# First stage of a cross-attention and expert kernel put in another order: key weights, row statistics, second normalised pair and the values of three batches

## What is computed

```python
def layer(x, ctx):
    q = layernorm(x) @ w_q.T + b_q             # 16 heads of 16 features
    k, v = split(ctx @ w_kv.T + b_kv)          # per batch: 77 keys, 77 values
    attn = softmax(q k^T / sqrt(16))           # per head, over the 77 keys
    x = x + (attn v) @ w_out.T + b_out
    # then 8 experts of 1024 hidden units, two per row, with a capacity per expert
    h = silu(rows_of_expert @ fc1_w.T + fc1_b)
    y = h @ fc2_w + fc2_b
    return x + layernorm_affine(layernorm(x) + gated sum of y)
```

## Time and profile before

| | |
|---|---|
| time, median of 3 runs | 838.27 us |
| lowest to highest | 837.16 to 839.23 us |
| the profiled execution's own time | 840.41 us |
| its span, first to last instruction | 838.6 us |
| mean granted TensorE clock | 0.905 of full |
| busy: TensorE | 699.2 us (83% of the span) |
| busy: VectorE | 583.7 us (70%) |
| busy: GpSimd | 435.0 us (52%) |
| busy: ScalarE | 395.3 us (47%) |

### The profile page before, as it was taken

One profiled execution on the slowest core, in us unless ns is written; L12 is line 12 of the kernel. 1 busy time (PEld: TensorE's weight loads), 2 busy tenths in 40 slices (PEclk: granted clock), 3 DMA queues, 4 the chain that ended last, 5 costly groups with the idle time before them and its releaser, 6 DMA issues.

```text
span 838.6 us, 16510 instructions
## 1 busy us (share of the span) xinstructions
PE 699.2 (83%) x5636; PEld 662.2 (79%) x5637; DVE 583.7 (70%) x1177; ACT 395.3 (47%) x899; POOL 435.0 (52%) x480
## 2 busy tenths in 40 slices
PE   3599999999999703499999995999969999999600
PEld 2489999899889602499999995999969999999600
DVE  2879888888877599375566666768657566764278
ACT  1255555555555312254455454555535444653264
POOL 3644554554653246625544656557556545542456
PEclk9599999999999855599999996999989999999855
DMA  9301101101101150214424545345443443332375
GB/s 291 126 14 39 36 29 39 38 28 38 39 29 36 52 156 0 60 32 101 91 41 101 102 100 107 52 101 106 101 104 52 95 91 52 53 46 26 35 231 175
DMA packets 55334, 63.91 MB, mean 76 GB/s; under 512 B 9296, under 2 KB 50512, under 8 KB 55120
## 3 DMA queue, kind: packets, MB, share of 16 engines
q0 software_dynamic: 15360, 21.31, 15.9%
q1 hardware_dynamic: 34784, 40.96, 14.9%
q10 hardware_dynamic: 5104, 0.44, 0.5%
HBM read 38.96 MB, written 23.72 MB: 75 GB/s over the span
## 4 chain that ended last, share of the span: by engine, by line
PE 79%; DVE 9%; issue 4%; DMA 3%; POOL 2%; ACT 1%; SPq 0%; DVEq 0%; ACTq 0%; POOLq 0%
PE banks L753 17%; PE banks L755 17%; PE banks L754 17%; PE banks L862 9%; PE banks L849 5%; PE banks L837 5%; PE banks L967 2%; PE banks L920 2%; POOL oh_id L531 2%; DMA sum_rows<-y_sb,slot_ids 1%; DVE z L1413 1%; PE banks L875 1%; DMA wv_sb<-in_wvT 1%; PE banks L782 1%; PE banks L910 1%
## 5 line engine op out<-in xcount | busy, mean ns | idle before, releaser
L509 POOL DMA_INDIRECT sum_rows<-y_sb,slot_ids x80 | 128.6, 1607 | 193.0 <-ACT y_sb L702 166.5
L712 ACT ACTIVATE hraw<-banks,b_now 128x256 f32<-128x256 f32 x320 | 132.5, 474 | 101.6 <-PE banks L755 101.5
L753 PE MATMUL banks<-xT_hi,w_hi 128*128 128x256 f32 x560 | 163.9, 293 | 0.2
L755 PE MATMUL banks<-xT_hi,w_lo 128*128 128x256 f32 x560 | 160.7, 287 | 0.0
L754 PE MATMUL banks<-xT_lo,w_hi 128*128 128x256 f32 x560 | 160.6, 287 | 0.0
L753 PE MATMUL banks<-w_hi,h_hi 128*128 128x256 f32 x528 | 148.9, 282 | 2.7 <-issue 2.7
L754 PE MATMUL banks<-w_lo,h_hi 128*128 128x256 f32 x528 | 148.6, 281 | 0.0
L755 PE MATMUL banks<-w_hi,h_lo 128*128 128x256 f32 x528 | 148.5, 281 | 0.0
L1357 DVE CAST h_hi<-hraw 128x512 fp32r<-128x512 f32 x160 | 75.6, 472 | 62.3 <-ACT hraw L712 62.0
L1359 DVE TENSOR_TENSOR h_lo<-hraw,h_hi 128x512 fp32r<-128x512 f32 x160 | 112.0, 700 | 5.5
L753 PEld LDWEIGHTS banks<-xT_hi,w_hi 128*128 128x128 f32 x560 | 108.9, 194 | 7.2 <-issue 7.2
(11 more groups left out here) (194 smaller groups left out, 1465.9 us busy)
## 6 DMA issues: line engine op xcount, KB each, us to landing
w1raw<-in_w1T SPq DMA_DIRECT2D x8, 1024.0 KB, 6.9
w2raw<-in_w SPq DMA_DIRECT2D x8, 1024.0 KB, 6.4
xn_rows<-xn SPq DMA_DIRECT2D x32, 128.0 KB, 1.7
sum_rows<-xn SPq DMA_DIRECT2D x32, 128.0 KB, 1.8
out<-z SPq DMA_DIRECT2D x16, 256.0 KB, 2.2
res<-sum_rows SPq DMA_DIRECT2D x7, 512.0 KB, 7.3
X<-in_x SPq DMA_DIRECT2D x2, 1280.0 KB, 14.2
xg<-xn_rows,slot_ids POOLq DMA_INDIRECT x80, 3.5
```

The costliest lines, as they stand in the source:

```text
L509: g.indirect_dma_start(sum_rows, bass.IndirectOffsetOnAxis(ap=slot_ids[:, st, 1, q:q + 1], axis=0), y_sb[:, u, q, :], None, bounds_check=N ...
L712: a.activation(hraw[:, j // 2, j % 2, :], banks[:, j // 2, (j % 2) * 256:(j % 2 + 1) * 256], ACT.Silu, bias=b1_now[:, (c // SPE) % 2, j:j ...
L753: t_.matmul(o, a_hi, b_hi, start=first, stop=False)
L755: return t_.matmul(o, a_lo, b_hi, start=False, stop=last)
```

## The change

- **Loads.** The key weights count on `load_ctx` instead of sharing a semaphore with the value weights. The order becomes context, keys, x tiles 0 to 3, query weights, value weights, output weights, the rest of x.
- **Keys.** TensorE waits for context and key weights only. Products go to banks PT and PV. ScalarE writes `kT_hi` directly from PSUM with the bias, VectorE makes `kT_lo` from PSUM, bias and `kT_hi` in one instruction; the tile `kT` and its rounding copy are gone.
- **Row statistics.** VectorE starts with the statistics of pair 0, then the low part of the query weights, then the normalisation of pair 0, then the statistics of pair 1; key and value work follows.
- **Second pair.** VectorE's `normalise_first(1)` is gone; GpSimd does it with two `centre` and two `scale` behind `spread_lo(0)`, followed by `bias(0)`, and only then the low keys of batches 1 to 3.
- **Values.** Before the first step only batch 0's values are made, biased and split. The products of batches 1 to 3 stand on TensorE behind the spreading of batch 0, between steps 0 and 1; their bias adds follow on VectorE there, their high and low parts in the hook between steps 1 and 2. The spreading of batch 0 goes round two banks instead of four.
- **ScalarE.** An exponential on a small tile comes early; the high query weights come before the keys; the copy of the key mask comes behind the first transposed pair.

```diff
-        V_BANKS = (PT, PV, TR, PJ)
+        V_BANKS = (PT, PV)
+
+        def v_products(b):
+
+            return banks[0:NK, (TR, PJ)[b // 2], (b % 2) * D:(b % 2 + 1) * D]
...
             sp.dma_start(ctx_sb[:], ctxT.rearrange("(c p) b k -> p c (b k)", p=P)).then_inc(load_ctx, 16)
-            sp.dma_start(wk_sb[:], wkT.rearrange("(c p) o -> p c o", p=P)).then_inc(load_wkv, 16)
+            sp.dma_start(wk_sb[:], wkT.rearrange("(c p) o -> p c o", p=P)).then_inc(load_ctx, 16)
             sp.dma_start(X[:, 0:4, :], x_t[:, 0:4, :]).then_inc(load_x[0], 16)
-            sp.dma_start(wv_sb[:], wvT.rearrange("(c p) o -> p c o", p=P)).then_inc(load_wkv, 16)
             sp.dma_start(wq_sb[:], wqT.rearrange("(c p) o -> p c o", p=P)).then_inc(load_wq, 16)
+            sp.dma_start(wv_sb[:], wvT.rearrange("(c p) o -> p c o", p=P)).then_inc(load_wv, 16)
+            sp.dma_start(wo_sb[:], woT.rearrange("(c p) o -> p c o", p=P)).then_inc(load_wo, 16)
             for n, (a, b) in enumerate(((4, 12), (12, 22), (22, NT))):
                 sp.dma_start(X[:, a:b, :], x_t[:, a:b, :]).then_inc(load_x[n + 1], 16)
-            sp.dma_start(wo_sb[:], woT.rearrange("(c p) o -> p c o", p=P)).then_inc(load_wo, 16)
...
             rstd_first(0)
-            pool.wait_ge(sem("kT_split"), 2 * DC)
+            rstd_first(1)
+            pool.wait_ge(sem("kT_split"), DC)
             spread_lo(0)
-            rstd_first(1)
...
+            pool.wait_ge(sem("xn1T_done"), 1)
+            for w in range(2):
+                centre(xn1[:, w, :], 2 + w, mv1[:, w, 0:1], "xn1_centred")
+            pool.wait_ge(sem("xn1_centred"), 2)
+            for w in range(2):
+                scale(xn1[:, w, :], rstd1[:, w:w + 1], "xn1_made")
+            pool.wait_ge(load_small, 16 * 4)
+            bias(0)
             for b in range(1, NB):
                 spread_lo(b)
...
+            act.wait_ge(sem("half_made"), 1)
+            a.activation(silu_warm[:], minus_half[:, 0:1], ACT.Exp)
+            act.wait_ge(load_wq, 16)
+            a.activation(wq_hi[:], wq_sb[:], ACT.Copy).then_inc(sem("w_hi_ready"), 1)
             act.wait_ge(load_small, 16 * 4)
             for f in range(DC):
                 act.wait_ge(sem("kT_done"), f + 1)
-                a.activation(kT[:, f, :], banks[:, f, 0:NB * NK], ACT.Identity, bias=bk_sb[:, f:f + 1])\
+                a.activation(kT_hi[:, f, :], banks[:, (PT, PV)[f], 0:NB * NK], ACT.Identity, bias=bk_sb[:, f:f + 1])\
                     .then_inc(sem("kT_made"), 1)
...
             first_layernorm(0)
-            act.wait_ge(sem("v_made"), NB)
-            a.activation(v_hi[:], v_sb[:], ACT.Copy).then_inc(sem("v_hi_made"), 1)
+            act.wait_ge(sem("masks_made"), 3)
+            a.activation(key_of_row_r[:], key_of_row[:], ACT.Copy).then_inc(sem("key_rows_made"), 1)
+            act.wait_ge(sem("v_made"), 1)
+            a.activation(v_hi[:, 0, :], v_sb[:, 0, :], ACT.Copy).then_inc(sem("v_hi_made"), 1)
             queries(0)
...
+            def later_values(b):
+                if b == 2:
+                    act.wait_ge(sem("v_made"), NB)
+                    a.activation(v_hi[:, 1:NB, :], v_sb[:, 1:NB, :], ACT.Copy).then_inc(sem("v_hi_made"), 1)
+
+            attention_steps(act, step, later_values)
...
-            pe.wait_ge(load_ctx, 16)
-            pe.wait_ge(load_wkv, 32)
+            pe.wait_ge(load_ctx, 32)
...
-            for b in range(NB):
+
+            def values_product(b):
                 for c in range(DC):
...
-            pe.wait_ge(sem("kT_made"), DC)
             first_layernorm(0)
+            pe.wait_ge(load_wv, 16)
+            values_product(0)
             pe.wait_ge(sem("wq_split"), 1)
             queries(0)
-            pe.wait_ge(sem("v_made"), NB)
...
                         spread(0, j, banks[0:JW, V_BANKS[j % len(V_BANKS)], 0:D])
+                    pe.wait_ge(sem("v_made"), 1)
+                    for n in range(1, NB):
+                        values_product(n)
...
+            def keys_lo(f):
                 dve.wait_ge(sem("kT_made"), f + 1)
-                v.tensor_copy(kT_hi[:, f, :], kT[:, f, :]).then_inc(sem("kT_split"), 1)
+                v.scalar_tensor_tensor(kT_lo[:, f, :], banks[:, (PT, PV)[f], 0:NB * NK], bk_sb[:, f:f + 1],
+                                       kT_hi[:, f, :].bitcast(f32), ALU.add, ALU.subtract)\
+                    .then_inc(sem("kT_split"), 1)
+
+            def values_biased(b):
+                dve.wait_ge(sem("v_done"), 1 if b == 0 else NB)
+                v.tensor_tensor(v_sb[:, b, :], v_products(b), bv_sb[0:NK, :], ALU.add).then_inc(sem("v_made"), 1)
+
+            def values_lo(b, n, made):
+                dve.wait_ge(sem("v_hi_made"), made)
+                v.tensor_tensor(v_lo[:, b:b + n, :], v_sb[:, b:b + n, :], v_hi[:, b:b + n, :].bitcast(f32), ALU.subtract)\
+                    .then_inc(sem("v_lo_made"), 1)
+
             dve.wait_ge(load_x[0], 16)
             row_stats(0)
             dve.wait_ge(sem("st1_made"), 2)
             aggregate(0)
...
             dve.wait_ge(sem("w_hi_ready"), 1)
             split(wq_hi, wq_lo, wq_sb, "wq_split")
+            normalise_first(0)
+            row_stats(1)
+            dve.wait_ge(sem("st1_made"), 4)
+            aggregate(1)
             dve.wait_ge(load_small, 64)
...
+            keys_lo(0)
             first_lo(0)
+            keys_lo(1)
+            values_biased(0)
             dve.wait_ge(sem("masks_made"), 3)
             for f in range(DC):
                 spread_keys(0, f)
...
             queries_lo(0)
-            row_stats(1)
-            dve.wait_ge(sem("st1_made"), 4)
-            aggregate(1)
-            normalise_first(1)
+            values_lo(0, 1, 1)
             dve.wait_ge(load_x[1], 16)
...
                 if u == 0:
+                    if i == 0:
+                        dve.wait_ge(sem("xn1_made"), 4)
                     aggregate(i + 2)
...
                     split(wo_hi, wo_lo, wo_sb, "wo_split")
+                    for n in range(1, NB):
+                        values_biased(n)
+                if b == 2:
+                    values_lo(1, NB - 1, 2)
                     for n in (2, 3):
                         dve.wait_ge(load_x[n], 16)
```

More of the change, by code:

```diff
@@ L414, in _, with bias, centre, scale @@
             rstd_first(0)
-            pool.wait_ge(sem("kT_split"), 2 * DC)
+            rstd_first(1)
+            pool.wait_ge(sem("kT_split"), DC)
             spread_lo(0)
-            rstd_first(1)
+            def bias(j):
+                if within(j, PAIRS):
+                    pool.wait_ge(sem("xn1_made"), 2 * j + 2)
+                    for v in range(2):
+                        xt = X[:, ds(2 * j + v, 1), :].rearrange("p a d -> p (a d)")
+                        g.tensor_tensor(xt, xt, bo_sb[:], ALU.add).then_inc(sem("x_biased"), 1)
+            def centre(out, tile, mean, name):
+                rows = X[:, ds(tile, 1), :].rearrange("p a d -> p (a d)")
+                g.tensor_tensor(out, rows, mean.to_broadcast([P, D]), ALU.subtract).then_inc(sem(name), 1)
+            def scale(out, rstd, name):
+                g.tensor_tensor(out, out, rstd.to_broadcast([P, D]), ALU.mult).then_inc(sem(name), 1)
+            pool.wait_ge(sem("xn1T_done"), 1)
[6 more added lines that the diff above has]
+            bias(0)
             for b in range(1, NB):
@@ L440, in _ @@
                    allow_small_or_imprecise_dtypes=True).then_inc(sem("route_consts"), 1)
[L442 to L458, removed]
             def step(i, u):
@@ L658, in step @@
                                  ACT.Copy).then_inc(sem("logits_made"), 1)
-            attention_steps(act, step)
+            def later_values(b):
[3 more added lines that the diff above has]
+            attention_steps(act, step, later_values)
             router_exp(1, LATE)
@@ L755, in mm3 @@
                 return t_.matmul(o, a_lo, b_hi, start=False, stop=last)
-            pe.wait_ge(load_ctx, 16)
-            pe.wait_ge(load_wkv, 32)
+            pe.wait_ge(load_ctx, 32)
             for f in range(DC):
                 for c in range(DC):
-                    m = t_.matmul(banks[:, f, 0:NB * NK], wk_sb[:, c, f * P:(f + 1) * P], ctx_sb[:, c, :],
+                    m = t_.matmul(banks[:, (PT, PV)[f], 0:NB * NK], wk_sb[:, c, f * P:(f + 1) * P], ctx_sb[:, c, :],
                                   start=(c == 0), stop=(c == DC - 1))
                 m.then_inc(sem("kT_done"), 1)
-            for b in range(NB):
+            def values_product(b):
                 for c in range(DC):
-                    m = t_.matmul(banks[0:NK, 2 + b // 2, (b % 2) * D:(b % 2 + 1) * D],
-                                  ctx_sb[:, c, b * NK:(b + 1) * NK], wv_sb[:, c, :], start=(c == 0), stop=(c == DC - 1))
+                    m = t_.matmul(v_products(b), ctx_sb[:, c, b * NK:(b + 1) * NK], wv_sb[:, c, :],
+                                  start=(c == 0), stop=(c == DC - 1))
                 m.then_inc(sem("v_done"), 1)
```

(18 more changed lines are left out.)

14 lines of the change are left out of this document (3 added, 11 removed).

## The result

| | median, us | lowest to highest | ratio to before, 95% interval |
|---|---|---|---|
| before (4 runs beside it) | 837.71 | 836.49 to 839.23 | |
| after (4 runs) | 830.85 | 830.14 to 831.60 | 0.9919 [0.9902, 0.9935] |

The change makes the kernel 6.9 us faster: 833.0 was forecast, with a range of 829.5 to 837.0. The profiled execution took 830.14 us, its span is 828.4, the mean granted clock 0.916 (before 0.905).

The account below looks back on a forecast made before the run. The front was taken as bound by VectorE and its order, with TensorE at half clock, and attention from about 48 us by TensorE. Terms −4.65 − 2.15 + 1.5 = −5.3 us gave a median of 833.0, range 829.5 to 837.0.

Parts of the forecast that it names:

- Start: First loads and key products: products start at 5.9 instead of 10.1 us, alone off the path; `rstd` there at 10.35.
- Normalising pair 0: VectorE's two `xn`: 0.36 us each without GpSimd beside them, instead of 1.27; done from 11.35 to 12.1.
- `xn` costs 1.27 by itself: Rival on VectorE's normalising: `xn` is no cheaper without GpSimd's `KH_lo` beside it; +1.8 us, 834.8; chance 10%.
- Spreading: Keys spread by VectorE and GpSimd from 15.3 us, taking turns, ending at 19.25; turns cost 0.4 us.
- Queries at half clock: First queries on TensorE, from 15.0 us: taken to last 2.94 us, with `q_hi` done at 18.85.
- Pair 1 on GpSimd: GpSimd normalises pair 1 from 19.25 in four pieces of 0.59 us, ready at 22.0, hidden by 1 us.
- Between the steps: Between steps 0 and 1: rounds over two banks +1.0 us, twelve value products 5.1; tile 1 scores at 34.0, −4.65.
- Step 1 and the clock: Attention step 1: clock full from 33.9 us, saving 2.65; VectorE's biases cost 0.5; together −2.15, step 2 at 41.45.
- Hook behind step 1: Before step 2's `vals`: ScalarE's copy and VectorE's `v_lo` delay them, leaving TensorE standing; +1.5 us, between 0 and 2.5.
- second spell at half clock: Rival: the pause of 1.5 us drops the clock again for 6.85 us, costing 3.4; 836.4; chance 17%.
- stay at 1.2 GHz: Rival for slower, from 34.0 us on: clock stays low; 843.0 us if it rises at 54; chance 6%.
- the default of half clock: Rival at the first key products: started earlier, they run at half clock and end at 13.7; 834.6 us; chance 5%.

Follow-up runs that it names:

- again: The changed kernel profiled and measured once more, unaltered: 830.41 us, 0.9912 of the kernel before.
- the loads alone: Kernel before with only the key weights counted on the context's semaphore, so key products need not wait for the value weights: 834.89 us, 0.9962.
- loads and statistics: Kernel before with key weights counted apart from value weights, and pair 0's row statistics ahead of VectorE's two rounding copies: 832.94 us, 0.9943.
- the value products in front: Changed kernel with the value products of batches 1 to 3 behind the first queries instead of between steps 0 and 1: 830.48 us, 0.9910.
- the padded pair: Kernels before and after, each with nine useless 128-column products at TensorE's very start, shifting the later code: 830.72 and 823.61 us.
- the padded kernel with the same nine: Changed kernel with late value work in idle time, nine useless products in TensorE's early waits, nine more at its start: 821.94 us, 0.9813.

## Why the prediction was right, point by point

| | predicted | after | again |
|---|---|---|---|
| first key product | 5.9 | 5.72 | 5.74 |
| `wq_lo` starts | 10.6 | 10.01 | 10.53 |
| two `xn` | 0.72 | 0.73 | 0.73 |
| scores of tile 0 | 20.25 | 18.37 | 19.30 |
| pair 1 transposed | 23.05 | 20.86 | 22.24 |
| scores of tile 1 | 34.0 | 30.80 | 32.83 |
| step 1 lasts | 7.45 | 7.42 | 7.42 |
| scores of tile 2 | 41.45 | 38.22 | 40.25 |
| step 2, over the 6.38 of before | +1.5 | +1.35 | +1.33 |

**Start: right in its times, incomplete in what it was worth.** In the new order the statistics wait for x alone (8.26), as said. That the shared semaphore had cost the old order 3.2 us, through VectorE's rounding of the keys, was not seen. The first profile was lucky in its query weights: in the ten profiles with the new order of loads, `wq_lo` starts between 10.01 and 11.18, and 10.01 is this one.

**Normalising pair 0: right.** The rival *`xn` costs 1.27 by itself* is refuted twice, by 0.73 for two here and by 0.72 for pair 1 on VectorE, while with the loads alone the same two cost 2.54 beside `KH_lo`, and with loads and statistics one ahead of it cost 0.40 and the next beside it 1.30.

**Spreading: mis-sized.** "GpSimd to 16.5, VectorE 17.25, GpSimd 18.5, VectorE 19.25" assumed turns with GpSimd first. In both profiles VectorE's two `KH_hi` ran through at 1.49 to 1.50, and GpSimd's two took 3.93 and 3.96, 1.46 more than alone, which is just the length of the two `KH_hi` ("alone" is loosely said: the 2.47 of before ran beside `xn`, and it was `xn` that waited). So they do exclude each other, but VectorE's second followed its first without a turn. The bound of step 0 moved from `q_lo` to `KH_lo`.

**Queries at half clock: wrong.** They ran at 1.00 in the profile shown first (13.70 to 15.4, 0.28 each), where 2.94 us at half clock had been taken. The clock was 1.00 up to 19.9. So `q_hi` and `q_lo` came early and `KH_lo` was the last to end. It started at 14.08 (again: 14.98) where 15.3 was forecast, which gives 1.2 (0.3) of the 1.9 us (0.95) by which tile 0 was better than the sum said; the rest is the missing turn and the early `q_lo`.

**Pair 1 on GpSimd: the right time, no worth.** It was ready at 20.6 (22.0 was forecast), ahead of its use, but VectorE would have had the room.

**Between the steps: right.** Twelve products took 4.72 us where 5.1 was forecast, the blocks went in rounds. From pair 1's transposes to the scores of tile 1 passed 9.94 and 10.59 us (predicted 10.95).

**Step 1 and the clock: right in length; the reason went deeper.** The clock was full before the step's scores in both profiles. What the prediction did not see is that the value products bought this: without them step 1 takes 9.1 to 9.9 us. With products without use added in the idle time it took 7.32 us in one profile and 8.79 in the other.

**Hook behind step 1: right.** +1.35 us, TensorE waiting 1.12 for `vals`, and it goes when the copy goes.

**Rivals.** No second spell at half clock followed the pause at 40.5, and the clock did not stay at 1.2 GHz. The first products ran at 1.00, 0.53 us each against 0.49 before, so the default of half clock that the Trainium skill names ("TensorE: Matmul & The Clock Gate", section "What's actually happening") did not meet them. Half clock did come soon behind them in some profiles of this front (0.51 between 12.8 and 16.3 us with the value products in front, scores of tile 0 at 19.78 instead of 18.37), but 1.15 of these 1.4 us stood there already at the first transposes (12.64 against 11.49), behind later query weights.

The forecast's mechanism held; its size was too small in one term. Up to the scores of tile 1 it had −4.65 us, and the profiles have −7.86 and −5.83; step 1 (−2.17 where −2.15 was said) and step 2 were right. The gain was 6.9 instead of 5.3 us.

Between tile 3 and the end the two profiled executions differ by another 1.5 us (10.2 in the span, 8.7 at tile 3); the profiled execution of before, 840.41, also lay 2.7 us above its median. In the padded pair, where the expert stage takes 402.6 us in both, the gain is 6.8 us at tile 3, 6.8 in the span (828.7 to 821.9) and 7.1 in the medians: the change's gain is that of the front. What stays open is why the clock holds in one execution of a front and not in the next, and which engine's instructions the pauses wait for.

## What to carry to other kernels

Ask of a late load not only who waits for it, but what stands behind the waiting instruction in the same engine's list: one shared semaphore here cost 3.2 us through row statistics that need neither of the two weights. Work put into a pause of TensorE, even work without use, can be worth more than its removal when the pause lets the clock fall ahead of a step bound by TensorE; look at more than one profile before you count on it. And before a difference of under 1% is put down to an edit, shift the code of both kernels by some instructions and measure again.

## What the runs showed of the hardware that was not expected

- **The position of the code.** Nine products at TensorE's start, in time that was idle, made three kernels faster by 6.0 to 7.5 us of some 830, and a fourth, as it seems, slower by 3.5. The differences lie in pauses of 2 to 6 us, most of which the profile gives as "issue", behind stretches that a branch skips. The Trainium skill, "Runtime: NRT & Kernel Launch", section "Instruction fetch mechanics", says that fetching ahead is purely sequential and that a taken branch to code outside what has been fetched makes the engine wait for a fetch. The traces agree in where the pauses stand, in that position matters, and in the packet of 16 KB on the instruction queue that is under way in each of the 49 pauses; no run measured a fetch by itself.
- **VectorE and GpSimd.** Two `KH_lo` beside two `KH_hi` took 3.93 us against 2.47 beside `xn`, while `KH_hi` lost nothing. The rule of the Trainium skill that the prediction used ("SBUF — State Buffer", section "Who interferes with whom") holds in the exclusion. The same section says that the order of issue decides who blocks; by the records GpSimd's pair began first (14.08 against 14.25) and waited all the same, so the trace does not bear that out for a queue of two.
- **The clock.** When it falls in the front differs between profiles of one kernel: at 19.9 us in one of the kernel after, at 18.5 in the other. In the first, TensorE had waited 3.0 us until 18.37; in the kernel with the value products in front the clock held until 26.5, behind waits of 1.38 and 2.21 us. How a front of short pauses will be clocked could be read from no single run; three products in one pause and six in the next kept it at 1.00 in one profile, and in the padded kernel with the same nine it fell at 28.6.
